# One language-model block on one core: the tensor engine's loop over blocks 1 to 6 written out

## The reference

```python
h = rms_norm(rms_norm(emb_table[x]) * norm_weight @ proj_weight.T)
n = layernorm(h)                       # attention over all 256 tokens of a row
q, k = feature_map(n @ Wq.T), feature_map(n @ Wk.T)    # 16 heads of 32
attn = causal((q @ k.T) ** 2);  o = attn @ v / (attn.sum(-1) + eps)
h = h + o @ Wo.T
x = fwht(layernorm(h) * SU_ug) / 64    # Walsh-Hadamard transform over 512
y = silu(x @ W_gate.T * wg) * (x @ W_up.T * wu)        # 2048 wide
h = h + (fwht(y * SU_dp) / 64 @ W_down.T) * wd         # transform over 2048
```

## Time and profile before

| | |
|---|---|
| median of three timed runs | 1380.29 us (1379.37 to 1381.31) |
| the profiled execution's own time | 1382.72 us |
| its span, first to last instruction | 1380.9 us |
| PE busy | 1262.6 us, 91% |
| DVE, ACT, POOL busy | 660.9, 398.2, 565.2 us |
| mean granted clock of PE | 0.972 |

### The profile page before, as it was taken

One profiled execution on the slowest core, in us unless ns is written; L12 is line 12 of the kernel. 1 busy time (PEld: TensorE's weight loads), 2 busy tenths in 40 slices (PEclk: granted clock), 3 DMA queues, 4 the chain that ended last, 5 costly groups with the idle time before them and its releaser, 6 DMA issues.

```text
span 1380.9 us, 18955 instructions
## 1 busy us (share of the span) xinstructions
PE 1262.6 (91%) x7257; PEld 619.9 (45%) x7257; DVE 660.9 (48%) x1154; ACT 398.2 (29%) x703; POOL 565.2 (41%) x483
## 2 busy tenths in 40 slices
PE   5564398999999999999999999999999999999999
PEld 3453155554444444444444444444444444444444
DVE  1654658782645463645355445535543645361110
ACT  4452354342133212330233113311332123211210
POOL 0343234442266424752276227632664256421220
PEclk9897689999999999999999999999999999999999
DMA  8913413311435234443344244433543445020000
GB/s 284 318 38 64 73 35 69 69 24 39 99 100 108 47 92 101 108 60 84 89 112 77 69 100 101 84 72 84 110 92 59 99 97 111 16 69 23 0 1 31
DMA packets 232720, 114.18 MB, mean 83 GB/s; under 512 B 197892, under 2 KB 215608, under 8 KB 232120
## 3 DMA queue, kind: packets, MB, share of 16 engines
q1 hardware_dynamic: 220160, 74.38, 26.2%
q0 software_dynamic: 11520, 37.76, 9.6%
q10 hardware_dynamic: 952, 0.75, 0.2%
HBM read 57.01 MB, written 9.70 MB: 48 GB/s over the span
## 4 chain that ended last, share of the span: by engine, by line
PE 76%; DVE 9%; issue 5%; DMA 4%; ACT 4%; POOL 2%; SPq 0%; DVEq 0%; POOLq 0%; ACTq 0%
PE bank L1178 23%; PE bank L1180 23%; PE bank L1179 23%; PE bank L1330 3%; DMA prod<-sg 2%; PE bank L1173 2%; DVE wd L568 1%; POOL p L408 1%; PE bank L1221 1%; DMA hid<-in_L_tok_norm_weight 1%; DVE wd L567 1%; DVE wgu L553 1%; DVE prod L765 1%; ACT p L951 1%; PE bank L1171 1%
## 5 line engine op out<-in xcount | busy, mean ns | idle before, releaser
L1178 PE MATMUL bank<-xT,wgu 128*128 128x512 f16 x1024 | 390.1, 381 | 9.7 <-issue 8.2
L1180 PE MATMUL bank<-xT,wgu 128*128 128x512 f16 x1024 | 389.9, 381 | 0.0
L1179 PE MATMUL bank<-xT,wgu 128*128 128x512 f16 x1024 | 389.8, 381 | 0.0
L470 POOL TENSOR_TENSOR hid<-a,hid 128x512 f16<-128x512 f32 x128 | 172.7, 1349 | 289.0 <-ACT hid L951 288.4
L839 DVE SCALAR_TENSOR_TENSOR a<-bank,kap,sg 128x512 f32<-128x512 f32 x128 | 96.1, 751 | 320.4 <-PE bank L1180 305.4
L1178 PE MATMUL bank<-wd,hid 128*128 128x512 f16 x512 | 194.1, 379 | 0.0
L1180 PE MATMUL bank<-wd,hid 128*128 128x512 f16 x512 | 194.0, 379 | 0.0
L1179 PE MATMUL bank<-wd,hid 128*128 128x512 f16 x512 | 194.0, 379 | 0.0
L951 ACT ACTIVATE hid<-a 128x512 f16<-128x512 f32 x128 | 80.9, 632 | 280.0 <-DVE a L839 280.0
L1178 PEld LDWEIGHTS bank<-xT,wgu 128*128 128x128 f16 x1024 | 100.7, 98 | 129.3 <-issue 14.6
L1180 PEld LDWEIGHTS bank<-xT,wgu 128*128 128x128 f16 x1024 | 100.5, 98 | 122.2 <-issue 2.2
(11 more groups left out here) (192 smaller groups left out, 1371.1 us busy)
## 6 DMA issues: line engine op xcount, KB each, us to landing
out<-a SPq DMA_DIRECT2D x24, 256.0 KB
wgu<-in_L_ffn_W_gate SPq DMA_DIRECT2D x16, 256.0 KB, 5.5
wgu<-in_L_ffn_W_up SPq DMA_DIRECT2D x16, 256.0 KB, 5.2
wd<-in_L_ffn_W_down SPq DMA_DIRECT2D x4, 1024.0 KB, 9.8
out<-h_row SPq DMA_DIRECT2D x8, 256.0 KB
hid<-att_table,ids_p POOLq DMA_INDIRECT x84, 3.5
xT<-in_L_tok_proj_weight SPq DMA_DIRECT2D x1, 1024.0 KB, 9.2
p<-in_L_attn_Wq SPq DMA_DIRECT2D x1, 1024.0 KB, 14.4
```

The costliest lines, as they stand in the source:

```text
L470: nc.gpsimd.tensor_tensor(hid[:, 1, s, :], a32[:, :], hid[:, 0, s, :], ALU.subtract)\
L1178: mm(dst, w[0], v[0], start=first, stop=False)
L1179: mm(dst, w[0], v[1], start=False, stop=False)
L1180: return mm(dst, w[1], v[0], start=False, stop=final)
```

## The change

PE's loop statement becomes a loop of the program that writes the program: its body is emitted six times, with b as a number. Waits in it have constant values. The order of PE's matmuls and the other engines' programs stay as they are.

```diff
             pe.wait_ge(S["y_done"], 3)
-            with pe.Fori(1, NB - 1) as b:
+            for b in range(1, NB - 1):
                 for s in range(SLOTS):
                     feed(b, s)
                     attend(b + 1, s)
```

## The result

The written-out kernel takes 1369.34 us (median of six runs, 1366.75 to 1369.82), the kernel before beside it 1379.15 us (six runs, 1377.04 to 1381.31). The ratio is 0.9919, 95% interval 0.9909 to 0.9930, so faster by 0.7 to 0.9%. (The ratio is not the quotient of the two medians, which is 0.9929.) Measured again later with other runs on both sides, it was 0.9935 (0.9919 to 0.9951). The forecast was 1370.5 us, which over its 1380.29 is 0.9929.

A forecast was written before the change was run, and what follows sets the result against it. PE's instruction stream with its holes was taken as the bound from about 250 us on. The median 1380.29 us less 9.75 for five taken branches, all other terms 0, gave 1370.5 us; range 1368.0 to 1374.5.

The forecast's parts named there:

- The five taken branches go, 9.75 us in full: At PE's five jumps back to the loop head, matmuls start late; removing these holes gains 9.75 us.
- The second way to the sum, 9.09 to 9.75: Five passes with a jump, 725.44 us, against five times the first, 716.35: 9.09 us, the term's lower bound.
- Instructions not there yet, second piece behind the head: Holes at PE's jumps are instructions not yet fetched; every jump costs two pieces more, the long hole 1.4 to 2.1 us.
- Written-out pieces cost nothing: Fetching PE's written-out passes, 7 pieces each, is hidden by work PE still holds; costed at nothing.
- The waits at L1330 and L1339 keep their size: PE's waits for POOL's product (L1330) and a transpose (L1339) stay unchanged, since both begin with something PE released.
- Registers become constants: 0: Dropping register arithmetic before waits in PE's loop body gains 0 to 1.8 us; taken as 0.
- The added wait: 0: At slot 1, `feed` newly waits for DVE's L847 of the block before; met 4 us before, costs nothing.
- ACT 0.1 us late at DVE, covered: At block starts ACT would make DVE 0.1 us late; four us of slack before PE's slot 2 cover it.
- The cheap jump: Rival: long holes belong to piece boundaries and stay; only short holes go, 0.96 us, time 1379.3; 5%.
- the starving program: Rival: written-out pieces come late, PE stands still 1.4 to 2.1 us each; all 42 would give 1442; 3%.
- ACT's delay: Rival: ACT's later block start gives back 1.54 us at each of five boundaries; gain 2.05 us, time 1378.2; 4%.

The follow-up runs named there:

- the head at 232: Kernel before with its loop kept, only PE's loop head placed at instruction 232 of a 256-instruction piece; ratio 0.9945 to the kernel before.
- loops that stay in memory: Three kernels keeping PE's loop, against the kernel before: early jump hint 0.9923, head at instruction 16 of a piece 0.9927, 32 idle instructions ahead of the loop 0.9933.
- the loop with the hint: Kernel before with its loop kept, plus one instruction at the body's head telling PE's sequencer early of the jump back; ratio 0.9923.

## Why the prediction was right, and where not

The step that failed is the one for everything ahead of the loop. The prediction says that all the change touches lies behind about 250 us, has no term for the stretch ahead of PE's loop, and leaves 0.7 us for it and for all other scatter: its terms alone reach down to 1368.7 us, and the range's lower end was set at 1368.0, although the 1 us that it names for the spread of the timed runs would have given 1367.7. What the runs showed in its place: the setup was 378.79 us in the first profile before and 374.97 in the first after, 3.8 us less, and over 17 profiles written-out kernels are 1.8 us shorter there in the mean, all of it in the wait for the first operand; whether by the change or by scatter stays open. The mechanism at the jumps was right; the rest follows part by part.

- *The five taken branches go, 9.75 us in full.* Right in mechanism: the holes are gone and the passes are 9.66 us shorter between the first two profiles. The size varies: the holes are 9.8, 7.8 and 9.4 us in the three profiles of the kernel before, and over three profiles of each the passes are 867.9 and 858.5 us in the mean, a gain of 9.5. That 9.75 came so close is in part luck, as the point on the pieces shows.
- *The second way to the sum, 9.09 to 9.75.* Both lie between the 7.8 and 9.8 us of holes in the three profiles.
- *Instructions not there yet, second piece behind the head.* Right, and shown by the hole that moved with the head at 232. What the prediction had not seen is why there was anything to fetch in a loop whose body can stay: it straddled one piece too many. The count of 9 pieces a pass stood in the earlier trace rows; I took it as given.
- *Written-out pieces cost nothing.* Wrong. None is late for PE itself, but one that arrives during a transpose delays that, by up to some 2 us, and in one or two passes of each profile PE waits for the end of the chain, mostly 1.2 to 1.6 us at L1330. The kernel before had the same kind of waits, so what the prediction left out on both sides cancels: the passes of loops that stay in memory are 11.0 us shorter than before (867.9 to 856.9), not 9.5.
- *The waits at L1330 and L1339 keep their size.* Right for L1339. For L1330 only by sum, which is chance: 0.57, 0.67, 0.38, 0.44, 0.63 and 0 us late before, 0, 0, 1.57, 0, 1.20 and 0 after, 2.7 and 2.8 together. The kernels that fetch nothing in their passes have 0 from the second pass on.
- *Registers become constants: 0.* Right. With registers in all waits, the loop with the hint has shorter passes than any written-out one.
- *The added wait: 0.* Right; no matmul of slot 1 waits.
- *ACT 0.1 us late at DVE, covered.* It was right to charge nothing, but not for the reason given: ACT's start moved back to 3.83 us, where 5.05 was taken over from behind a jump, and DVE is not late at all.
- *The rivals.* The cheap jump fell with the profile after, which has no hole six matmuls into a block, and with the loops whose jumps take 0.2 us and leave no hole either; the starving program didn't come about, though the collisions with transposes are its mild form; ACT's delay wasn't there.
- *The range.* 9.75 us were forecast. The first ratio gives 1379.15 × 0.0081 = 11.2 us, the second 1380.01 × 0.0065 = 9.0. The first, taken off the median beside it, is 1367.98, just outside the range's lower end of 1368.0, while the median measured, 1369.34, is inside. By the medians the forecast fits: its starting point, 1380.29, was the median of three runs, the six runs beside the written-out kernel have 1379.15, and that less 9.75 is 1369.40. A gain of 9.5 us in the passes and 1.8 in the setup would be 11.3, which meets the first ratio and not the second. How much of the 1.4 us too many is a shorter setup and how much is scatter stays open, for the timed runs have no profile.

## What to carry to other kernels

When the engine that bounds the kernel runs a loop, look at its branch instructions and at how many instruction pieces a pass fetches, before anything is written out. Here branches of microseconds and pieces in every pass meant that the body didn't stay. A hint for the jump or a head in another place was worth as much as writing the loop out, and spared the fetches, which otherwise landed among the transposes. When the first cause is gone, read the waits again: the next one, an order of two DMAs, was worth another half per cent. And give the range of a forecast what one kernel's own runs scatter, the part ahead of the change included: here that was 4 to 8 us between the shortest and the longest run of the kernel before.

## What was unexpected of the hardware

- A loop body of about 1700 instructions on PE was fetched anew in each pass, or in one pass of five, or not at all, by where its head lay: 70 pieces with the head at 243, 34 at 104, 25 at 19. The 32 idle instructions that moved the head from 243 to 19 gained 0.67% (0.50 to 0.84).
- A branch taken back to the loop's head took PE's sequencer 0.21 to 0.26 us when its target was still there and 3.3 to 3.9 us when not.
- A transpose of 3.25 us took 4.6 us in the median when an instruction piece of 16 KB for PE arrived with it (12 against 128 transposes of one execution), and up to 5.3 in other profiles; where no piece arrived between 520 and 1230 us, none took over 3.9. The cost shows two engines further on.
